# Setup of a fused transformer block: query fuse pieces first, row split and remaining pieces reordered

## What is computed

```
mod = (silu(c) @ wmod).reshape(8, 6, 1, 256)      # sa, ca, ga, sb, cb, gb
ga, gb = sign(g) * max(|g|, 0.25)                  # the two gates
h = layernorm(x) * (1 + ca) + sa
x = x + ga * attention(h)      # q = (h @ w_dq.T) @ [w_qr; w_uq].T, k from w_kr and w_dkv, 16 heads
h = layernorm(x) * (1 + cb) + sb
x = x + gb * moe(h)            # 8 groups, top 8 of 32, silu(gate) * up, down
```

## Time and profile before

| | |
|---|---|
| median of three runs | 1102.49 us |
| profiled execution, its own time | 1101.17 us |
| its span (first to last instruction) | 1099.2 us |
| mean granted TensorE clock | 0.98 |
| PE busy / weight loads | 1016.1 us (92%) / 723.9 us (66%) |
| DVE, ACT, POOL busy | 770.1, 401.3, 412.8 us |
| chain that ended last | PE 78%, DVE 7%, issue 7%, POOL 4% |

### The profile page before, as it was taken

The page is one execution under the profiler, slowest core; times in us unless marked ns, Lnnn a source line. Parts: engine busy times, 40 slices in busy tenths (PEclk is TensorE's granted clock), DMA queues, the critical chain, the costliest instruction groups (busy, mean ns, idle before and its releaser), DMA issues.

```text
span 1099.2 us, 24746 instructions
## 1 busy us (share of the span) xinstructions
PE 1016.1 (92%) x9744; PEld 723.9 (66%) x9744; DVE 770.1 (70%) x1516; ACT 401.3 (37%) x723; POOL 412.8 (38%) x349
## 2 busy tenths in 40 slices
PE   6979989999899989999899998999999998999678
PEld 4546667766676667766677666766677766776456
DVE  6767687585957868677785859678686777857344
ACT  4335433254314443145331543144431453314310
POOL 1526342264505353154422635054430544326100
PEclk9989989999999999999999999999999999999969
DMA  6220000200002000200002000020002000010000
GB/s 190 58 88 2 3 1 1 68 2 2 1 4 66 2 1 1 69 2 2 1 1 69 2 2 1 2 69 2 1 1 68 2 2 1 1 49 2 2 1 20
DMA packets 22233, 23.59 MB, mean 21 GB/s; under 512 B 6315, under 2 KB 20139, under 8 KB 22131
## 3 DMA queue, kind: packets, MB, share of 16 engines
q1 hardware_dynamic: 22130, 22.02, 6.6%
HBM read 17.80 MB, written 4.21 MB: 20 GB/s over the span
## 4 chain that ended last, share of the span: by engine, by line
PE 78%; DVE 7%; issue 7%; POOL 4%; ACT 2%; DMA 1%; DVEq 0%; POOLq 0%; SPq 0%; ACTq 0%
PE ring L1124 17%; PE ring L981 12%; PE ring L982 10%; PE ring L983 10%; PE ring L1196 8%; PE av L1140 6%; PE ring L1104 6%; PE ring L1095 2%; DVE mcol L863 2%; PE ring L1112 1%; PE ring L1185 1%; PE ring L1042 1%; ACT pt L672 1%; POOL rows L553 1%; POOL prod L547 1%
## 5 line engine op out<-in xcount | busy, mean ns | idle before, releaser
L672 ACT ACTIVATE pt<-ring 128x384 f32<-128x384 f32 (+1 forms) x384 | 170.8, 531 | 329.6 <-PE ring L1124 293.4
L562 POOL TENSOR_SCALAR_AFFINE_SELECT pt<-pt 128x512 f32<-128x512 f32 x128 | 79.7, 638 | 413.1 <-ACT pt L672 413.1
L863 DVE TENSOR_REDUCE mcol<-ring 128x1 f32<-128x128 f32 (+3 forms) x512 | 212.2, 481 | 19.3 <-PE ring L1104 17.8
L839 DVE TENSOR_TENSOR prod<-ring,table 128x1024 f32<-128x1024 f32 x128 | 155.3, 1217 | 97.7 <-PE ring L983 97.0
L1124 PE MATMUL ring<-rows 32*128 32x512 f32 (+3 forms) x3072 | 165.4, 329 | 18.4 <-ACT pt L672 8.5
L553 POOL TENSOR_TENSOR rows<-prod,rows 128x1024 fp32r<-128x1024 f32 x64 | 152.6, 2394 | 36.7 <-ACT rows L652 36.7
L1124 PEld LDWEIGHTS ring<-rows 32*128 32x128 f32 x3072 | 120.0, 185 | 69.4 <-issue 33.1
L546 POOL TENSOR_TENSOR prod<-prod 128x512 f32<-128x512 f32 x64 | 82.6, 1290 | 134.8 <-DVE prod L839 134.4
L652 ACT ACTIVATE rows<-prod 128x1024 fp32r<-128x1024 f32 x64 | 67.1, 1061 | 60.3 <-PE ring L1124 39.3
L1140 PE MATMUL av<-pt,vals 128*17 128x512 f32 (+3 forms) x1024 | 84.7, 436 | 3.3 <-POOL pt L562 3.2
L1196 PE MATMUL ring<-dn,pt 128*128 128x256 f32 x384 | 85.0, 381 | 0.0
(11 more groups left out here) (162 smaller groups left out, 1609.2 us busy)
## 6 DMA issues: line engine op xcount, KB each, us to landing
xn<-x_dram SPq DMA_DIRECT2D x8, 512.0 KB, 4.0
xr<-x_dram SPq DMA_DIRECT2D x8, 512.0 KB, 3.7
out_dram<-xr SPq DMA_DIRECT2D x8, 512.0 KB, 3.2
gate_bc<-gates_scratch SPq DMA_DIRECT2D x8, 256.0 KB, 4.9
pt<-wmod_dram SPq DMA_DIRECT2D x1, 1536.0 KB, 6.5
pt<-gup_t_dram SPq DMA_DIRECT2D x16, 96.0 KB, 2.6
dn<-wu_t_dram SPq DMA_DIRECT2D x1, 640.0 KB, 10.1
xr<-wk_t_dram SPq DMA_DIRECT2D x1, 512.0 KB, 8.2
```

Source lines behind the costliest of these rows:

```text
L672: sc.activation(pt[:, PT_AT[n] + h * w:PT_AT[n] + (h + 1) * w], ps[:, 0:w], ACT.Exp, scale=SCALE).then_inc(exp_ready.sem, 1)
L839: ve.tensor_tensor(prod[:, s % PROD, :, :], ps[:, :].unsqueeze(1).broadcast_to([P, 2, S]), table[:, :, :], ALU.mult).then_inc(rotated.sem, 1)
L863: last = ve.reduce_max(mcol[:, q, h * HR + HD:h * HR + HD + 1], ps[:, at:at + (q + 1) * P], AX_X)
```

## The change

The loads of the first two fuse pieces (`w_dq` and columns 0 to 511 of `wu_t`) and the group numbers are issued ahead of the modulation weights; the other columns come as DMAs of their own behind the router's weights, with a semaphore of their own (`ld_rest`). `spread` is the first step, then `fuse.0` and `fuse.1`, then `silu` and the rest up to the projections. The `gates` step is parted: PE's matmuls keep their place after `turn1`, and DVE's part is a step of its own, `gates_out`, behind `rotate.0011`; `low1` thus comes ahead of it. SP waits for the gates' matmuls (`full_sem`) where it waited for their read. `split_uv` stands behind the first two projections, `combine.001` ahead of `lo.000`, `fuse.2` and `fuse.3` behind the first group's projections, `fuse.4` and `fuse.5` among those of the second group, and `values` behind `shifted.00`. The body is as it was.

```diff
--- before.py
+++ after.py
@@ -66,18 +66,19 @@
     out = []
     for token in text.split():
         kind, args = token.split(".")
-        out.append((kind, *map(int, args)))
+        out.append((kind, *(int(i) for i in args)))
     return out
 
 
 
 SETUP_ORDER = """
-latent.0 latent_hi.0 latent_lo.0 fuse.1 rope.0000 rotate.0000 rope.0001 rotate.0001 combine.000 kcon.00 kcon_hi.00
-kcon_lo.00 rope.0010 rotate.0010 rope.0011 rotate.0011 hi.000 lo.000 combine.001 fuse.2 fuse.3 hi.001 lo.001
-rope.0100 rotate.0100 qcon.00 qcon_hi.00 qcon_lo.00 rope.0101 rotate.0101 combine.010 values.00 values_out.00
-values.01 values_out.01 kcon.01 kcon_hi.01 kcon_lo.01 hi.010 maxima.000 reduce.000 lo.010 rope.0110 rotate.0110
-maxima.001 reduce.001 rope.0111 rotate.0111 combine.011 maxima.002 reduce.002 fuse.4 fuse.5 qcon.01 qcon_hi.01
-qcon_lo.01 shift.00 shifted.00 hi.011 lo.011 spread. split_ffn.0 split_ffn.1
+spread. fuse.0 fuse.1 silu. stats1.0 pow1.0 split_d. norm1.0 mod. split_k. turn1.00 turn1.01 gates. modulate1.00
+low1.00 modulate1.01 low1.01 latent.0 latent_hi.0 latent_lo.0 rope.0000 rope.0001 split_uv. rotate.0000 rotate.0001
+combine.000 rope.0010 rope.0011 rotate.0010 hi.000 rotate.0011 gates_out. kcon.00 kcon_hi.00 kcon_lo.00 combine.001
+lo.000 fuse.2 fuse.3 hi.001 lo.001 qcon.00 qcon_hi.00 qcon_lo.00 rope.0100 rotate.0100 rope.0101 rotate.0101
+combine.010 maxima.000 reduce.000 fuse.4 rope.0110 rotate.0110 hi.010 lo.010 maxima.001 reduce.001 rope.0111
+rotate.0111 combine.011 fuse.5 maxima.002 reduce.002 kcon.01 kcon_hi.01 kcon_lo.01 qcon.01 qcon_hi.01 qcon_lo.01
+hi.011 lo.011 shift.00 shifted.00 values.00 values_out.00 values.01 values_out.01 split_ffn.0 split_ffn.1
 """
 BODY_ORDER = """
 load_next.1 loads.0 maxima.010 rope.0200 reduce.010 score.000 rotate.0200 rope.0201 exp.000 rotate.0201 maxima.011
@@ -124,12 +125,6 @@
 """
 
 
-def setup_steps():
-    out = [("silu",), ("stats1", 0), ("pow1", 0), ("norm1", 0), ("mod",), ("split_d",), ("split_k",), ("turn1", 0, 0), ("turn1", 0, 1),
-           ("gates",), ("modulate1", 0, 0), ("low1", 0, 0), ("modulate1", 0, 1), ("low1", 0, 1), ("fuse", 0), ("split_uv",)]
-    return out + steps_of(SETUP_ORDER)
-
-
 def ring_places(steps):
 
     place, n = {}, 0
@@ -144,7 +139,7 @@
     return place, n
 
 
-SETUP, FIRST, LAST = setup_steps(), steps_of(BODY_ORDER), steps_of(LAST_ORDER)
+SETUP, FIRST, LAST = steps_of(SETUP_ORDER), steps_of(BODY_ORDER), steps_of(LAST_ORDER)
 PLACES = {}
 for _name, _steps in (("setup", SETUP), ("body", FIRST), ("last", LAST)):
     PLACES[_name] = ring_places(_steps)
@@ -251,8 +246,8 @@
         av = ctx.enter_context(nc.psum_tensor("av", [P, 512], F32))
 
 
-        ld_wo, ld_d, ld_mod, ld_q, ld_k, ld_tab, ld_small, ld_ffn, ld_down, ld_idx = (
-            sem(n) for n in ("ld_wo", "ld_d", "ld_mod", "ld_q", "ld_k", "ld_tab", "ld_small", "ld_ffn", "ld_down", "ld_idx"))
+        ld_wo, ld_d, ld_mod, ld_q, ld_rest, ld_k, ld_tab, ld_small, ld_ffn, ld_down, ld_idx = (
+            sem(n) for n in ("ld_wo", "ld_d", "ld_mod", "ld_q", "ld_rest", "ld_k", "ld_tab", "ld_small", "ld_ffn", "ld_down", "ld_idx"))
         x_loaded = Count(sem("x_loaded"), 1, 16)
         res_loaded = Count(sem("res_loaded"), 1, 16)
         gate_loaded = Count(sem("gate_loaded"), 1, 16)
@@ -323,7 +318,7 @@
         tanh_c_ready, keys_hi_ready, fuse_hi_ready, ffn_hi_ready = (
             sem(n) for n in ("tanh_c_ready", "keys_hi_ready", "fuse_hi_ready", "ffn_hi_ready"))
         cst_ready = sem("cst_ready")
-        N_SMALL = 7
+        N_SMALL = 5
 
         def full_value(b, part, place):
 
@@ -443,31 +438,34 @@
 
 
             sp.dma_start(idx_sb[:, :], chosen).then_inc(ld_idx, 16)
+            for copy in range(2):
+                sp.dma_start(grp_i[copy * NX:(copy + 1) * NX, :], groups).then_inc(ld_idx, 16)
+            sp.dma_start(wdq_st[:, 0, :], w_dq[0:P, :]).then_inc(ld_q, 16)
+            sp.dma_start(wdq_st[0:CQ - P, 1, :], w_dq[P:CQ, :]).then_inc(ld_q, 16)
+            sp.dma_start(wu_main[:, 0:512], wu_t[0:P, 0:512]).then_inc(ld_q, 16)
+            sp.dma_start(wu_rest[:, 0:512], wu_t[P:CQ, 0:512]).then_inc(ld_q, 16)
             sp.dma_start(ct[:, :, :], c_t.rearrange("(c p) b -> p c b", p=P)).then_inc(ld_mod, 16)
             sp.dma_start(wmod_st, wmod.rearrange("(c p) n -> p c n", p=P)).then_inc(ld_mod, 16)
             sp.dma_start(xn[:, :, :], x_rows(0, 0)).then_inc(x_loaded.sem, 16)
             sp.dma_start(wd_st, wdkv_t.rearrange("(c p) n -> p c n", p=P)).then_inc(ld_d, 16)
             for c in range(EC):
                 sp.dma_start(wk_st[c], wk_t[c * P:(c + 1) * P, :]).then_inc(ld_k, 16)
-            sp.dma_start(wdq_st[:, 0, :], w_dq[0:P, :]).then_inc(ld_q, 16)
-            sp.dma_start(wdq_st[0:CQ - P, 1, :], w_dq[P:CQ, :]).then_inc(ld_q, 16)
-            sp.dma_start(wu_main, wu_t[0:P, :]).then_inc(ld_q, 16)
-            sp.dma_start(wu_rest, wu_t[P:CQ, 0:NG * NROPE]).then_inc(ld_q, 16)
-            sp.dma_start(wu_rest_con, wu_t[P:CQ, NG * NROPE:NQ]).then_inc(ld_q, 16)
             for copy in range(2):
                 half = slice(copy * CKV, (copy + 1) * CKV)
                 sp.dma_start(wuk_st[half, :], wuk_t).then_inc(ld_small, 16)
                 sp.dma_start(wuv_st[half, :], wuv_t).then_inc(ld_small, 16)
-                sp.dma_start(grp_i[copy * NX:(copy + 1) * NX, :], groups).then_inc(ld_small, 16)
             sp.dma_start(gw_st, gw_t.rearrange("(c p) n -> p c n", p=P)).then_inc(ld_small, 16)
+            sp.dma_start(wu_main[:, 512:], wu_t[0:P, 512:NQ]).then_inc(ld_rest, 16)
+            sp.dma_start(wu_rest[:, 512:], wu_t[P:CQ, 512:NG * NROPE]).then_inc(ld_rest, 16)
+            sp.dma_start(wu_rest_con, wu_t[P:CQ, NG * NROPE:NQ]).then_inc(ld_rest, 16)
             for i, t in enumerate((cos_t, sin_t)):
                 for h in range(HG):
                     sp.dma_start(table[h * HR:(h + 1) * HR, i, :], t.rearrange("(d h) s -> h d s", h=HG)[h, :, :])\
                       .then_inc(ld_tab, 16)
 
-            sp.wait_ge(ld_idx, 16)
+            sp.wait_ge(ld_idx, 48)
             sp.wait_ge(mod_read, 1)
-            sp.wait_ge(gates_read, 1)
+            sp.wait_ge(full_sem, full_value(0, "setup", PLACES["setup"][0][("gates",)]))
             chosen_at = [sp.value_load(idx_sb[0:1, g:g + 1], min_val=0, max_val=NX - 1) for g in range(G)]
             for g in range(G):
                 src = gup_t[bass.ds(chosen_at[g], 1), :, :].rearrange("o (c p) (a i) -> p (o c) a i", p=P, a=2)
@@ -755,9 +753,9 @@
                         for c in (2, 6):
                             last = ve.tensor_scalar(modT[:, c:c + 2, :], modT[:, c:c + 2, :], 1.0, None, ALU.add)
                         last.then_inc(mod_ready, 1)
-                    elif kind == "gates":
-
-                        ps = wait_full(ve, b, part, step)
+                    elif kind == "gates_out":
+
+                        ps = wait_full(ve, b, part, ("gates",))
                         ve.wait_ge(keys_split, 1 + EC)
                         ve.tensor_scalar(gates, ps[0:B, :], 0.0, 2.0, ALU.is_ge, ALU.mult)
                         chain(ve.tensor_copy(gates_abs, ps[0:B, :]))
@@ -769,7 +767,7 @@
                                                 ALU.add, ALU.mult).then_inc(gates_ready, 1)
                     elif kind == "spread":
 
-                        ve.wait_ge(ld_small, 16 * N_SMALL)
+                        ve.wait_ge(ld_idx, 48)
                         ve.wait_ge(pool_setup, 4)
                         chain(ve.tensor_copy(gid, grp_i[:, :]))
                         ve.tensor_scalar(spread[:, :].rearrange("p (g i) -> p g i", g=G),
@@ -1024,7 +1022,9 @@
                         last.then_inc(full_sem, 1)
                     elif kind == "fuse":
                         if step[1] == 0:
-                            pe.wait_ge(ld_q, 80)
+                            pe.wait_ge(ld_q, 64)
+                        if step[1] == EC:
+                            pe.wait_ge(ld_rest, 48)
                         ps = take_bank(pe, b, part, step)
                         ec, c0, n = FUSE[step[1]]
                         tail_rows = wu_rest[:, c0:c0 + n] if c0 < NG * NROPE else wu_rest_con
```

## The result

The changed kernel takes 1107.93 us (median of 5 runs, 1107.78 to 1109.65) against 1102.49; the ratio, formed from all the runs and not from the two medians, is 1.0057, 95% interval [1.0042, 1.0071]. It is slower, as forecast, but by 5.4 us where the sum said 2.3, and just beyond the top of the forecast's range, 1107.8. The profiled execution took 1107.80, with a span of 1105.8 and a mean clock of 0.977.

The account below looks back on a forecast made before the run. It took PE to bound the batch loop, so setup costs whatever delays PE's first scores. `score.000` 0.4 us sooner plus 2.7 us of clock loss gave +2.3, put on the median 1102.49: 1104.8 us, range 1100.8 to 1107.8.

Parts of the forecast that it names:

- the sum: Whole kernel: 0.4 us gained by `score.000` and 2.7 charged for the clock, +2.3 us in all.
- The first pieces' duration: Start of PE: `fuse.0` at 6.7, four matmuls at 1.02 us for two, `mod` at 12.7, 3.9 us late.
- the third rival, slow start: First fuse pieces, or `mod` behind them, run at 1.2 GHz: +4.2 us, 1106.7 to 1109; chance 0.17.
- The new wait: At `fuse.2`, PE idles 6 us for the gates' bank; `maxima.000` 1.8 us late, plus 2.7 for the clock.
- B's loss: From the experiments' theory B: the gates' chain amid the rotations costs PE's pause and what follows.
- the forecast's 49 with the clock: `maxima.000` starts at 46.8 us or, if the clock falls in PE's pause, at 49.
- Behind `maxima.000`: Pieces among projections spare DVE half of 3.8 us of waits (1.9); `shifted.00` at 61.1, `score.000` 0.4 sooner.
- `spread`'s 2.4 us: End of setup: DVE's gap from moving `spread`; only 0.3 us gained, as DVE waits for ACT's copy for `gu_lo`.
- The price of the last stand: PE's wait before `score.000`, about 4.3 us, stays, and so does its clock cost of 2.7 us.
- The rival of the lighter end: All 2.4 of `spread` gained, stand before `score.000` under 3 us, no clock fall there: -3.1, 1099.4; chance 0.13.

Follow-up runs that it names:

- e4: The kernel before with 30 extra bf16 matmuls of 256 columns on PE ahead of its first step, results not read: 1117.43 us, ratio 1.013.
- e1: The changed kernel with `gates_out` back ahead of the projections, right behind `low1.01`: 1102.48 us, ratio 0.9997 to the kernel before.
- e7: The changed kernel with the gates' two bank-reading operations ahead of the projections, the other three left late: 1104.64 us, ratio 1.0026 to the kernel before.
- e5: The kernel before with 30 extra matmuls of 2 columns ahead of PE's first step, results not read: 1116.16 us, ratio 1.0117.
- e9: The kernel before with only `spread` and its loads moved to the start: 1102.74 us, ratio 1.0006.
- e2: The changed kernel with 24 extra matmuls ahead of PE's first piece, results not read: 1114.7 us, ratio 1.0116 to the kernel before.
- e6: The changed kernel with 12 extra matmuls of 512 columns ahead of PE's first piece: 1103.95 us, ratio 1.0014 to the kernel before.
- e3: e1 with `fuse.0`, `fuse.1` and their loads behind the modulation again: 1099.36 us, ratio 0.9965 to the kernel before.
- e8: e3 with `fuse.2` and `fuse.3` moved ahead of `hi.000`: 1097.29 us, ratio 0.995 to the kernel before.
- e10: The kernel before with the changed order from `maxima.000` to the end of the setup, `spread` left in place: 1097.12 us, ratio 0.9953.

## Why the prediction was wrong in size

**The first pieces' duration.** This is the term that failed first. `fuse.0` starts at 6.95, forecast 6.7. The pairs were priced at 1.02 from a row at 26 us and took 2.07, so `mod` is 4.1 late against the forecast, and that 4.1 arrives nearly whole at `low1` (28.21 for 24.1) and `rotate.0000` (34.55 for 30.6). This is the third rival, slow start, with its price of 4.2 and its 1106.7 to 1109. It was held down to a chance of 0.17 by the 1.00 of the earlier trace rows, which says nothing: e4 shows that PE was at 1.2 GHz in that very stretch of the kernel before. The Trainium skill ("TensorE: Matmul & The Clock Gate", "What's actually happening"), by whose rule throttled is the default, was right, and the reading of the row against it was wrong.

**The new wait.** Its place, releaser and length were right: PE idle from 36.7 to 42.09, 5.4 us for the 6 forecast, and the clock fell with it. But the step followed only the bank. It let `qcon.00` come 4.1 us after `fuse.2`, as before; without any gates in the way it comes 7.6 after it (36.32 to 43.94 in e1), since the rotations now stand ahead of `wq_lo` on DVE. And the three operations behind the two reads were not counted as standing ahead of `kcon_lo` and `wq_lo`, nor was it counted that they meet POOL there. They take 5.0 us (42.04 to 47.01) for 1.77 alone, and in e7 they are worth nearly half of B's loss. `maxima.000` at 55.48 is 6.5 us beyond the forecast's 49 with the clock; 4.0 of that is the start.

**Behind `maxima.000`.** To `shifted.00` it takes 14.36 us, 1.8 less than the 16.18 of before, forecast 1.9; from there to `score.000` 0.64 less, forecast 0.3. That `spread`'s 2.4 us would not be gained was right, and for the reason given: DVE waits 1.88 us for ACT's `gu_hi` in its stead.

**The price of the last stand.** "The stand before `score.000` stays and so does its price" was half wrong. It stays, at 4.08 us, but costs 3.5 us less up to the first store. The rival of the lighter end had 2.7 for this, by way of a stand under 3 us and of `spread`; the runs show another way. With two short waits ahead of it the low stretch behind the stand is 6.8 us (before, e4, e5, e9), without them 3.4 (all the others), whether the stand is 4.0 or 4.4. By the price given at the end, that is about a third of the 3.5 us. The rest is a second low stretch, at 154 us; first the window of before, then that of the changed kernel, which has no low stretch from 81.5 to 289:

```profile
154.00:155.00 1.00, 0.79 (x8) 0.63 (x12) 1.00 (x3) 0.00 (x0) 0.56 (x1) 0.50 0.00 0
```

```profile
154.00:155.00 1.00, 1.00 (x6) 0.90 (x5) 0.97 (x2) 0.00 (x0) 1.00 (x1) 1.00 0.00 0
```

It is 6.8 in the kernel before, e4, e5 and e9, 3.4 in e1, e2, e6 and e7, and missing in the changed kernel, e3, e8 and e10. Why is open. Those four have a low stretch at 276 to 289 us instead, which the other kernels lack, so part of this gain seems only put off to a later batch.

So there are two gains and two losses. The forecast saw 0.35 of the 4.30 us that the start costs, 3.6 of the 6.15 of the new wait, nearly all of the gain behind `maxima.000` and nothing of the 3.5 behind the score. That the total came as near as it did is luck: the unseen gain makes up for more than half of the unseen losses.

## What to carry to other kernels

An instruction that is moved takes the clock of its new place: compare durations of the same shape there, and don't trust a clock column that has not yet moved. An operation taken off one engine's path must be followed into the queue that it joins, all its instructions and what the neighbour engine does beside them, not only the semaphore that it holds. A change that loses can hold a good part: timing its parts one at a time found two versions at 1097, some 10 us under the whole.

## What the runs showed of the hardware

**DVE beside POOL.** The stretched operations end a fixed time after POOL's operation does. The one that takes 0.68 alone ends 0.54 after it in the changed kernel (43.81, POOL 43.27) and 0.55 in e7 (44.43, POOL 43.88); the one that takes 0.41 ends 0.28 after it (46.30, POOL 46.02) and 0.27 in e7 (42.75, POOL 42.48). So each was held until POOL was nearly through and then took its own time; they did not run at half speed. In e7 POOL was held as well: its operation of 40.84 begins while DVE's of 40.68 runs, and takes 1.64 for 1.26. The Trainium skill ("SBUF — State Buffer", "SBUF: two separate sides") says that the port pair the two share is an exclusive lock; these rows agree. The gates' first two operations, which read PSUM, keep their 0.67 beside POOL.

**Instructions ahead of the loop.** 30 more matmuls of 2 columns at the start cost 13 us (e5). In five passes of the batch loop PE pauses 1.9 us at the same place with nothing to wait for, each pause ending 1.1 to 1.6 us after the pass before issued its store, and the clock falls more often. 12 more matmuls bring no such pause (e6). The sign to look for is a row "issue" at a line of the loop that the kernel before lacks. The Trainium skill ("Runtime: NRT & Kernel Launch", "Instruction fetch mechanics") has a stall in fetching code where a taken branch leads out of what is at hand; no run here shows whether this is one.

**What a low stretch costs.** From `score.000` to the first store the same work takes 128.0 us with one low stretch of 3.4 us (after, e3, e8, e10), 129 with two (e1, e2, e6, e7) and 131.1 to 131.6 with two of 6.8 (before, e4, e5, e9): about 1.0 to 1.2 us for each 3.4.
